# Feed-forward of an adapter and FFN kernel: GpSimd's scatters and gathers one by one instead of in bursts

## The reference

```python
w = weight[adapter_ids]
y = jnp.einsum('bsi,boi->bso', x, w)
t = y.reshape(b * l, Dm)[:, perm].reshape(b * l, h, d)
t = jnp.einsum('bhd,hdm->bhm', t, up)
t = jax.nn.gelu(t, approximate=False)
t = jnp.einsum('bhm,hmd->bhd', t, down)
out = x + t.reshape(b * l, h * d)[:, argsort(perm)].reshape(b, l, Dm)
```

## Time and profile before

| | |
|---|---|
| median of 3 runs | 292.39 us |
| the profiled execution's own time | 292.55 us |
| its span | 290.8 us |
| PE busy | 285.3 us, 98% |
| DVE busy | 186.1 us, 64% |
| ACT busy | 161.0 us, 55% |
| POOL busy | 102.1 us, 35% |
| granted TensorE clock, mean | 0.997 of full |

### The profile page before, as it was taken

One profiled execution on the slowest core, in us unless ns is written; L12 is line 12 of the kernel. 1 busy time (PEld: TensorE's weight loads), 2 busy tenths in 40 slices (PEclk: granted clock), 3 DMA queues, 4 the chain that ended last, 5 costly groups with the idle time before them and its releaser, 6 DMA issues.

```text
span 290.8 us, 4409 instructions
## 1 busy us (share of the span) xinstructions
PE 285.3 (98%) x1694; PEld 215.9 (74%) x1694; DVE 186.1 (64%) x219; ACT 161.0 (55%) x179; POOL 102.1 (35%) x96
## 2 busy tenths in 40 slices
PE   8999999999999999999999999999999999999994
PEld 7889898898898898898898998846364554636451
DVE  3788777767867859978959956635526273562323
ACT  4758228228227237447346350496785959668380
POOL 2000000008774001983000336157577773432514
PEclk9999999999999999999999999999999999999998
DMA  7999969889999999799988396563557672212203
GB/s 206 370 419 417 417 245 364 312 333 354 408 417 407 417 414 377 273 341 406 414 316 270 107 329 197 219 184 143 163 176 208 215 219 108 110 63 85 108 36 144
DMA packets 23796, 77.88 MB, mean 268 GB/s; under 512 B 2784, under 2 KB 11360, under 8 KB 18912
## 3 DMA queue, kind: packets, MB, share of 16 engines
q1 hardware_dynamic: 7056, 43.39, 38.4%
q0 software_dynamic: 7584, 25.18, 25.0%
q10 hardware_dynamic: 9136, 9.05, 9.0%
HBM read 60.82 MB, written 16.78 MB: 267 GB/s over the span
## 4 chain that ended last, share of the span: by engine, by line
PE 95%; DMA 1%; SPq 1%; POOL 1%; issue 0%; DVE 0%; ACT 0%; POOLq 0%; DVEq 0%
PE ps L572 38%; PE ps L582 20%; PE ps L633 19%; PE ps L610 6%; PE ps L613 5%; PE ps L616 5%; PE ps L548 3%; DMA w_raw<-w 1%; PE ps L553 1%; POOL out_rows L288 1%; SPq L200 1%; DVE w_raw L478 0%; SPq L228 0%; ACT w_hi L380 0%; POOLq L308 0%
## 5 line engine op out<-in xcount | busy, mean ns | idle before, releaser
L572 PE MATMUL ps<-x_pair,w_hi 128*128 128x512 f32 x480 | 111.6, 390 | 0.0
L572 PEld LDWEIGHTS ps<-x_pair,w_hi 128*128 128x128 f32 x480 | 89.1, 188 | 17.9
L332 ACT ACTIVATE w_hi<-w_raw 128x1024 fp32r<-128x1024 f32 x58 | 58.0, 1049 | 37.2 <-PE ps L572 22.6
L270 POOL DMA_INDIRECT t_raw<-y_rows,idx x32 | 40.8, 1276 | 99.2 <-DMA y_rows<-y_out 84.1
L435 DVE TENSOR_TENSOR w_lo<-w_raw,w_hi 128x1024 fp32r<-128x1024 f32 x60 | 70.6, 1220 | 1.4 <-PE ps L553 1.4
L361 ACT ACTIVATE hidden<-ps 128x1024 f32<-128x1024 f32 x56 | 53.9, 1030 | 24.5 <-PE ps L616 23.5
L464 DVE TENSOR_REDUCE y_out<-ps 128x256 f32<-128x512 f32 x64 | 42.4, 687 | 36.0 <-PE ps L582 35.7
L582 PEld LDWEIGHTS ps<-x_pair,w_lo 128*128 128x128 f32 x480 | 59.6, 192 | 1.2
L582 PE MATMUL ps<-x_pair,w_lo 128*128 128x256 f32 x480 | 59.9, 283 | 0.0
L633 PE MATMUL ps<-hidden,down_sb 128*64 128x512 f32 (+1 forms) x264 | 56.7, 582 | 0.0
L633 PEld LDWEIGHTS ps<-hidden,down_sb 128*64 128x64 f32 x264 | 18.2, 137 | 34.7 <-issue 25.6
(11 more groups left out here) (29 smaller groups left out, 147.7 us busy)
## 6 DMA issues: line engine op xcount, KB each, us to landing
w_raw<-w SPq DMA_DIRECT2D x29, 1024.0 KB, 7.4
y_rows<-y_out ACTq DMA_DIRECT2D x32, 256.0 KB, 9.1
x_raw<-x_cols SPq DMA_DIRECT2D x7, 1024.0 KB, 8.3
w_raw<-w SPq DMA_DIRECT2D x4, 256.0 KB, 4.4
w_raw<-w SPq DMA_DIRECT2D x2, 512.0 KB, 7.3
t_raw<-up SPq DMA_DIRECT2D x1, 1024.0 KB, 7.5
down_sb<-down SPq DMA_DIRECT2D x1, 1024.0 KB, 12.6
w_raw<-w SPq DMA_DIRECT2D x2, 384.0 KB, 6.0
```

Source lines behind the costliest of these rows:

```text
L270: nc.gpsimd.indirect_dma_start(t_raw[:, f % TG, :], None, y_rows[0:D * (chunk + 1), :], rows_of(f)).then_inc(t_in[f % TG], 16)
L332: nc.scalar.activation(w_hi[:, g % WS, k, :], w_raw[:, g % WRAW, k, :], ACT.Copy).then_inc(w_hi_done, 1)
L572: last = nc.tensor.matmul(y_bank(g, o), w_hi[:, ws, k, col], x_pair[:, xs, k, :, :], start=(k == 0), stop=False)
```

## The change

Only POOL's order in the feed-forward changes. After the four gathers of t for units 16 to 19 there is one scatter, one gather of t and, for f of 6 to 11, one gather of x rows for unit f + 4, in turns. The number of instructions, their sizes and their waits stay as they are; the other engines' programs do not change. From line 298 on, line numbers after are one or more smaller.

```diff
-            for j in range(GROUPS):
-                for f in range(TG + GROUP * j, TG + GROUP * (j + 1)):
-                    if f < NF:
-                        gather_t(f)
-                for f in range(GROUP * j, GROUP * (j + 1)):
-                    scatter(f)
-                if j == 1:
-                    for f in range(XR, LATE):
-                        gather_rows(f)
+            for f in range(GROUP):
+                gather_t(TG + f)
+            for f in range(NF):
+                scatter(f)
+                if TG + GROUP + f < NF:
+                    gather_t(TG + GROUP + f)
+                if XR <= f + GROUP < LATE:
+                    gather_rows(f + GROUP)
```

## The result

The kernel after takes 298.04 us (median of 5 runs, 297.52 to 298.08), the kernel before beside it 292.65 us: a ratio of 1.0181 with a 95% interval of 1.0166 to 1.0196, so 5.4 us slower. The profiled execution took 297.52 us with a span of 295.7 us, 4.9 us more than the span before. The forecast was 297.2 us, 4.8 over before. So the measured time is 0.1 us above the forecast's own range (296.1 to 297.9); the loss of 5.4 us is inside the range that it was built from (3.7 to 5.5), since the kernel before took 0.26 us more beside it than the 292.39 us that the forecast started from.

What follows compares the result with a forecast made beforehand. PE, busy 98% of the span, bounds the kernel, so POOL's order can only add waits. Stalls of 2.0 and 2.8 us make 4.8; 292.39 + 4.8 = 297.2 us, own range 296.1 to 297.9, with the clock's case 296.0 to 299.2.

Steps and rivals of the forecast that it cites:

- Parts 1 and 2: POOL idles about 195 to 199.7 ahead of gather 20, at no direct cost; gather 24 starts at 213.1, ahead of row gathers.
- Part 3: POOL's row gathers: 1.275 us a step from gather 24; unit 15's issued at 238.6, landing 3.6 us later at 242.2.
- The low end of the range: Smaller-loss rival, 8%: gather 24 at 212.6 and landings of 3.3 us end add 15 at 242.05, a loss of 3.7 us.
- the main sum: Add 15 ends at 242.9; wakes and first matmul pair make 243.2, against 238.4 before: 4.8 us lost, both stalls included.
- Part 4: PE's up layer waits for late adds at block 3 of groups 3 and 4: stalls of 2.0 and 2.8 us.
- the first stall: PE at block 3 of group 3 waits for unit 11's add, from 225.7 to 227.7: 2.0 us.
- the second: PE at block 3 of group 4 waits for add 15: 2.8 us, near 240.4.
- what I had as a rival: Clock falls at the second stall's end, slowing the remaining up phase: 0 to 3.4 us more, 298.9 us; chance 14%.
- the prediction's own signs of being wrong: Last row gather issued before 234 or landing under 3 us; clock under 1.00 between 225 and 250; PE waits in groups 5 to 7.
- Part 5: Behind group 4 POOL catches up by scatter 16, and the 4.8 us are neither given back nor added to.
- The estimate of 2.6 us: Skill's price for a 256 KB row gather, about 2.0 us plus bytes over 436 GB/s; loss would be 3.8 us.
- The other rivals: Rows arrive in time if POOL's 0.30 us gap goes, 292.4 us, 4%; spreading transfers gains something, 2%.

Runs made afterwards that it cites:

- experiment 1: Kernel after, but row gathers of units 10 to 14 in one piece behind scatter 4, unit 15's behind scatter 5: 292.39 us, ratio 1.0001 (second run).
- (2): POOL's bursts of four as in the kernel before, but row gathers of units 10 to 15 one a turn behind scatters: 292.57 us, ratio 1.0004 (second run).
- experiment 3: Kernel after with each row gather one turn sooner: 296.08 us, ratio 1.0114 (second run); two turns sooner: 292.55 us, ratio 1.0006.
- experiment 5: Kernel after, but row gathers of units 12 to 15 follow unit 11's in one piece, leaving only the first stall: 295.44 us, ratio 1.0094 (second run).
- experiment 7: Kernel after with each row gather one turn later: 304.53 us, ratio 1.0437.
- experiment 4: Kernel after, but within a turn the row gather stands ahead of the gather of t: 298.88 us, ratio 1.0236.
- the long pause: Kernel after, but row gathers 10 to 14 early behind scatter 4, unit 15's behind scatter 14, leaving one long stall: 302.28 us, ratio 1.0335.

## Why the prediction was right, and where it was off

**What holds PE up: right.** The place of the six row gathers is the whole cause. With them early, taking turns is free (experiment 1), and with POOL's bursts back, spreading them is free (2). Moving the last one by 1, 2 and 4 steps sooner takes the loss, in the runs in which the clock did not fall, to 4.45, 2.6 and 0.1 us, from 5.4 with a covered fall.

**Parts 1 and 2: right.** POOL's wait ahead of gather 20 was 4.93 us. Gather 24 was to start 27.76 us behind the start of the feed-forward (213.10 - 185.34), and did (212.47 - 184.71 = 27.76).

**Part 3: two terms a little small.** From gather 24 to the row gather of unit 15 the 20 steps took 26.01 us, not 25.5: most steps were 1.25 to 1.30, and two gathers of t took 1.14 and 1.25 us instead of 0.97. The landing took 3.76 us, not 3.6. That is 0.5 + 0.16 of the 0.6 to 0.8 by which the loss was larger than 4.8. The low end of the range was added up wrongly, which made no difference: the end of add 15 at 242.05 still needs the 0.3 us of wakes and first pair that the main sum has, so it gives 3.95 us and not 3.7.

**Part 4: the first stall was right, the second was not what I wrote.** The first wait was 2.0 us, as forecast. The second was forecast at 2.8 us and was 1.4. In between stood what I had as a rival: the clock fell. I had put it in the second stall, as the longer one, and priced it at 0 to 3.4 us. It fell behind the first, and its 3.4 us at half speed cost 1.5 us (eight pairs start 0.425 us apart instead of 0.235): the down layer of group 3 started at 232.26, 3.8 us later than 229.07 - 0.63. Yet it cost nothing in the end, since the last row gather set the time of group 4 by itself; PE only came to the wait later. Without the 1.5 us the second wait would have been about 2.9 us (1.36 + 1.5, an estimate), near the 2.8 forecast. The clock under 1.00 between 225 and 250 was also one of the prediction's own signs of being wrong, and it came; it did not touch the sum. That is why the sum of 4.8 stood although one of its stalls was wrong.

**Part 5: right.** Groups 5 to 7 have no wait, 12.68 us for a group (253.71 to 266.39), and POOL has caught up at scatter 16.

**The rule on a transfer's time.** The six row gathers after landed in 3.4 to 4.1 us, like the earlier trace rows. The estimate of 2.6 us from the Trainium skill (DMA: Bandwidth & Descriptors, Anatomy of one DMA) was 0.8 to 1.5 us too short for them; the rows of the trace were the right price.

**The other rivals.** POOL's gap of 0.30 us stayed where kinds alternate, so the rows could not be in time. Nothing gained.

## What to carry to other kernels

When an engine's hand-written queue is put into finer turns, look for the step with a deadline and count what now stands ahead of it, idle time included: here the last row gather came 19.5 us later than before (238.48 + 0.63 - 219.64, with the 0.63 us by which the feed-forward began sooner), some 14 us of which were slack (the 19.5 less the loss), and behind that each step of 1.275 us came out nearly one for one at the end. A wait in a strict queue costs nothing by itself; it costs what queues up behind it, and that can feed back if the wait is on the engine that is being starved. And where several waits follow one another, the last deadline decides: what lies ahead of it, a fallen clock too, is covered, and repairing half of it can show the other half bare.

## What the runs showed of the hardware

- The length of a pause of TensorE inside dense work did not by itself tell whether the clock fell. With one kernel on one chip the mean clock was 1.000 in three runs and 0.994 in three (experiment 3, a pause of 2.62 us in the profiled run), and the fall cost 1.85 us. It fell around pauses of 2.0 us (the kernel after) and 2.1 us (experiment 5), and at the end of one of 1.62 us that had one of 1.00 us shortly ahead of it (experiment 7), but not in one of 2.88 us (experiment 4). With a pause of 7.2 us it fell in all five runs.
- The fall can come after the work has resumed: 1.3 us behind the pause in the kernel after; in experiment 3 (one turn sooner) it came 2.1 us into the pause, in experiment 5 at the end of a pause of 2.1 us.
- The clock was at half for 3.4 us in the profiled runs of the kernel after, of experiment 3 and of experiment 5. With the long pause it was at half for 10.2 us, 6.0 us of which were dense work (245.04 to about 251.1).
- Transfers on POOL's queue now and then took 1.1 to 1.5 us to issue instead of 0.97, the scatter at 208.4 to 209.2 in most of these kernels among them. The cause stays open.
